# Laying out the scores and messages of an edge pass with the window's slots innermost

## The chip, the cores and the metric

The program runs on one core of one Trainium2 chip. The metric is device time in microseconds (us); the median of three runs of the kernel before is 3240.64 us (3236.63 to 3243.51). Engines are named as the profile names them: PE (TensorE matmul), PEld (its weight load), DVE (VectorE), ACT (ScalarE), POOL (GpSimd), SP (SyncE, which only issues transfers here).

## The reference

The model has two layers on x[128 graphs, 128 nodes, 128 features]: an attention layer over each graph, a mixture of 8 experts, a second attention layer, and a second mixture of 4 experts whose gates come from a graph attention over 524288 edges. Only that last gate is touched here:

```python
h = (x_flat @ W_gat).reshape(M, HEADS, NUM_EXPERTS)          # 4 heads x 4 experts
src = concatenate([edge_index[0], loops]); dst = concatenate([edge_index[1], loops])
a_src = (h * att_src).sum(-1); a_dst = (h * att_dst).sum(-1)
e = leaky_relu(a_src[src] + a_dst[dst], negative_slope=0.2)
e_max = segment_max(e, dst); ee = exp(e - e_max[dst])
denom = segment_sum(ee, dst); alpha = ee / (denom[dst] + 1e-16)
agg = segment_sum(h[src] * alpha[:, :, None], dst).reshape(M, 16) + b_gat
scores = layernorm(agg).reshape(M, HEADS, NUM_EXPERTS).mean(1)
# top 2 of 4 experts, softmax of their scores, weighted sum of gelu(x@W1+b1)@W2+b2
```

## The kernel before

Until about 1780 us of the span the kernel does both attention layers, the first mixture of experts and, between them on VectorE, a sort of all edges by destination. The rest is one function, `edges_and_experts1`, and all that changes lies in it.

After the sort, an edge's row has 20 floats: the 16 values h of its source (`GAT`) and the 4 scores a_src (`ROW` = 20 with them). A node's row `node[:, n, ROW:TAB]` has the 4 scores a_dst. Two pipelines run side by side.

*Gathers on POOL.* Edges are taken in parts of 2048, 16 per lane. `gather(u)` (L1508) issues 16 indirect transfers per part, each fetching one edge row for each of the 128 lanes into `edge_rows`; SP writes a finished part to the DRAM table `edge_table` in sorted order. POOL's loop does two parts (32 gathers), and then `windows` (L1514): two more indirect transfers that fetch for each lane a *window*, 40 consecutive sorted edge rows (`WINDOW` = 40), for each of two node pairs, into `win[P, 2, 40*20]`. POOL issues in order. The two window transfers wait for `picked` and `win_free`, which VectorE gives during the turn before.

*Turns on VectorE.* One `turn` handles a unit of 4 rows per lane (`UNIT` = 4: two pairs with two mates each, `PAIRS` = `MATES` = 2). It waits for its window, then: L1381 adds the two score terms into `sc`; L1383 to L1390 apply the leaky relu and put -1e30 on slots outside a row's edges (`hide`); L1393 takes the maximum over the 40 slots; L1400 subtracts it; ScalarE takes exp (L1594, waits for `scored`, gives `exped`); L1407 multiplies h by the weights into `msg`; L1411 and L1416 sum weights and messages over the slots; L1417 to L1458 make the gates from small tiles; L1470 adds up the four experts' outputs, which TensorE and ScalarE have made in the meantime (L1636, L1590, L1640, L1643). There are 32 turns. The first 31 each wait for windows that POOL fetches between gathers; the gathers have ended when the 31st runs, and its window transfers are followed by those of the last, 32nd turn, which POOL issues once `win_free` is given after L1416 has been issued.

In `sc` the order before is row, slot, head, and in `msg` row, slot, column, so the sums and maxima over slots read every 4th or every 16th float. The order of instructions on each engine is as written; no scheduler moves them. `step` adds to a semaphore, `settle` waits until all steps so far are done, `then` is both.

Of the kernel before, what the change touches and what calls it, by code (L numbers as in the profile page):

```python
# [6 lines left out]
ALU = mybir.AluOpType  # L7
# [5 lines left out]
AX_X = mybir.AxisListType.X  # L13

P = 128
# [27 lines left out]
HEADS = 4  # L43
TOP_EXPERTS = 4
GAT = HEADS * TOP_EXPERTS
ROW = GAT + HEADS
TAB = ROW + HEADS
WINDOW = 40
# [4 lines left out]
UNIT = 4  # L53
UNITS = GRAPHS // UNIT
MATES = 2
PAIRS = UNIT // MATES
# [9 lines left out]
BIG = 1e30  # L66
# [1085 lines left out]
def edges_and_experts1(nc, sem, a, x, rstd, shift, node, found, counted, source_ids, row_id, table_dram, edges_dram, out, ident, ones):  # L1152
# [5 lines left out]
    E = TOP_EXPERTS  # L1158
    SPAN = UNIT * NODES
    ROOT_GUESS = float(0x5F3759DF)  # L1160
    with ExitStack() as ctx:
        def sb(name, shape, dt=F32):
            return ctx.enter_context(nc.sbuf_tensor(name, shape, dt))
# [16 lines left out]
        win, win_ids = sb("win", [P, PAIRS, WINDOW * ROW]), sb("win_ids", [P, PAIRS], U32)  # L1180
# [4 lines left out]
        sc, hide = sb("win_score", [P, UNIT, WINDOW, HEADS]), sb("win_hide", [P, UNIT, WINDOW])  # L1185
        newtop, fade = sb("win_top", [P, UNIT, HEADS]), sb("win_fade", [P, UNIT, HEADS])
        msg, got, sums, adv = sb("win_msg", [P, UNIT, WINDOW, GAT]), sb("win_got", [P, UNIT, GAT]), sb("win_sums", [P, UNIT, HEADS]), sb("win_adv", [P, PAIRS])
# [50 lines left out]
        def _(dve):  # L1238
# [106 lines left out]
            FULL, HALF_FULL = [P, UNIT, WINDOW, HEADS], [P, PAIRS, WINDOW, HEADS]  # L1345
            w = win[:, :, :].rearrange("p t (k c) -> p t k c", c=ROW)
            w_flat = win[:, :, :].rearrange("p t (k c) -> p (t k) c", c=ROW)
            flat = sc[:, :, :, :].rearrange("p t k h -> p (t k h)")
            by_head = sc[:, :, :, :].rearrange("p t k h -> p t h k")
# [11 lines left out]
            def turn(came, unit, theirs, after):  # L1361
                mine, pair, after = bass.ds(unit * UNIT, UNIT), bass.ds(unit * PAIRS, PAIRS), bass.ds(after * PAIRS, PAIRS)
                mates = [bass.ds(unit * UNIT + m * PAIRS, PAIRS) for m in range(MATES)]
# [3 lines left out]
                def step(ins):  # L1367
                    ins.then_inc(step_s, 1)
                    done[0] += 1
# [4 lines left out]
                def then(ins):  # L1374
                    step(ins)
                    settle()
# [3 lines left out]
                for m in range(MATES):  # L1380
                    step(dve.tensor_tensor(sc[:, m * PAIRS:(m + 1) * PAIRS, :, :], w[:, :, :, GAT:ROW],  # L1381
                                           node[:, mates[m], ROW:TAB].unsqueeze(2).to_broadcast(HALF_FULL), ALU.add))
# [7 lines left out]
                step(dve.scalar_tensor_tensor(sc[:, :, :, :], hide[:, :, :].unsqueeze(3).to_broadcast(FULL), -BIG, sc[:, :, :, :], ALU.mult, ALU.add))  # L1390
                step(dve.tensor_scalar(adv[:, :], left[:, last_mates], 0.0, float(WINDOW), ALU.is_gt, ALU.mult))
                settle()
                step(dve.tensor_reduce(newtop[:, :, :], by_head, AX_X, ALU.max))  # L1393
# [6 lines left out]
                step(dve.tensor_tensor(sc[:, :, :, :], sc[:, :, :, :], newtop[:, :, :].unsqueeze(2).to_broadcast(FULL), ALU.subtract))  # L1400
# [4 lines left out]
                for m in range(MATES):  # L1405
                    of_mate = slice(m * PAIRS, (m + 1) * PAIRS)
                    step(dve.tensor_tensor(msg[:, of_mate, :, :].rearrange("p t k (h e) -> p (t k) h e", h=HEADS),  # L1407
                                           w_flat[:, :, 0:GAT].rearrange("p k (h e) -> p k h e", h=HEADS),
                                           sc[:, of_mate, :, :].rearrange("p t k h -> p (t k) h").unsqueeze(3).to_broadcast([P, PAIRS * WINDOW, HEADS, E]),
                                           ALU.mult))  # L1410
                step(dve.tensor_reduce(sums[:, :, :], by_head, AX_X, ALU.add))  # L1411
# [4 lines left out]
                step(dve.tensor_reduce(got[:, :, :], msg[:, :, :, :].rearrange("p t k c -> p t c k"), AX_X, ALU.add))  # L1416
# [407 lines left out]
```

## Time and profile before

| | us |
|---|---|
| median of 3 runs | 3240.64 |
| profiled execution, its own time | 3238.14 |
| its span, first to last instruction | 3236.1 |
| DVE busy | 2264.2 |
| PE busy | 1841.2 |
| POOL busy | 1806.9 |
| ACT busy | 1207.0 |
| 32 turns begin at 1875.26 and end with the span | 1360.8 |

The profile is of one execution. Its page lists the busy time of each engine, then groups of instructions; the trace behind it can be asked for groups by line and form, for waits (who was idle, and what ended it), for single lines, and for a timeline of one engine, where the start and the length of each instruction stand. Adjacent instructions of one line are merged there (x2), and a number in brackets is the idle time ahead.

### The profile page before, as it was taken

What the parts mean: (1) busy time and instruction counts of PE and PEld (TensorE: products, weight loads), DVE (VectorE), ACT (ScalarE), POOL (GpSimd) and SP (SyncE); (2) the same over time, 40 slices, a digit from 0 to 9 for tenths busy, and PEclk for the clock granted to TensorE, in tenths of its full rate; (3) what the DMA queues carried; (4) which work ended last, traced back from release to release, by engine and by line L of the source; (5) the groups of instructions that cost most, each with busy time, mean ns of one, the idle gap of its engine ahead of it and who ended that gap; (6) DMA issues with size and microseconds to landing.
All of it is one profiled execution on the core that took longest, in us unless ns stands there. A gap on an engine that the chain in (4) does not pass through costs nothing. (4 is left out here: it accounts for less than half of the span.)

```text
span 3236.1 us, 31753 instructions
## 1 busy us (share of the span) xinstructions
PE 1841.2 (57%) x9062; PEld 1287.2 (40%) x9117; DVE 2264.2 (70%) x4413; ACT 1207.0 (37%) x2449; POOL 1806.9 (56%) x1723
## 2 busy tenths in 40 slices
PE   0687764207777776366895325555555555545455
PEld 0466664205555444256785113322232333222233
DVE  7698978698888789977772355565666555656666
ACT  2576775414443433144783112222222222222222
POOL 4200024863544434254676777777777777777771
PEclk9998885559998988677895667777777777777777
DMA  6992000100111110121111111222112212221221
GB/s 236 291 393 106 4 19 24 39 27 23 39 46 32 45 39 14 49 67 49 48 36 35 34 40 41 43 43 41 32 41 43 43 41 43 43 41 30 43 43 34
DMA packets 169701, 192.40 MB, mean 59 GB/s; under 512 B 59193, under 2 KB 126048, under 8 KB 168960
## 3 DMA queue, kind: packets, MB, share of 16 engines
q1 hardware_dynamic: 107184, 118.69, 11.1%
q0 software_dynamic: 57088, 62.48, 9.5%
q10 hardware_dynamic: 5328, 9.97, 0.8%
q8 instruction: 52, 0.85, 0.1%
q14 instruction: 49, 0.40, 0.0%
HBM read 91.70 MB, written 105.25 MB: 61 GB/s over the span
## 5 line engine op out<-in xcount | busy, mean ns | idle before, releaser
L1508 POOL DMA_INDIRECT edge_rows<-node_table,edge_ids x1024 | 992.5, 969 | 313.5 <-issue 288.0
L1135 POOL DMA_INDIRECT token_results<-arena,token_of x160 | 247.9, 1550 | 362.6 <-ACT arena L1065 273.1
L579 DVE TENSOR_TENSOR sort_ping<-sort_pong 128x2048 f32<-128x2048 f32 (+1 forms) x238 | 407.1, 1751 | 48.1 <-ACT sort_pong L1003 43.4
L579 DVE TENSOR_TENSOR sort_pong<-sort_ping 128x2048 f32<-128x2048 f32 (+1 forms) x238 | 407.0, 1751 | 39.9 <-ACT sort_ping L1003 35.4
L1128 POOL DMA_INDIRECT slots<-arena,send x128 | 179.2, 1400 | 420.7 <-ACT arena L1022 385.3
L1630 PE MATMUL x_b_featT<-ident,x_feat 128*128 128x128 f32 x128 | 34.8, 428 | 630.3 <-PEq L1233 630.3
L1148 POOL DMA_INDIRECT adjacent<-keys,row_ids x256 | 249.2, 974 | 179.5 <-issue 78.9
L1381 DVE TENSOR_TENSOR win_score<-win,masked 128x320 f32<-128x320 f32 x64 | 28.6, 489 | 452.7 <-DMA win<-edge_table,win_ids 451.5
L1636 PE MATMUL x_b_hid<-x_featT,x_w 128*128 128x512 f32 x512 | 310.1, 759 | 28.3 <-PEq L1233 28.3
L1643 PEld LDWEIGHTS x_b_res<-x_w,x_hid 128*128 128x128 f32 x2048 | 243.5, 195 | 97.2 <-issue 97.2
L1630 PEld LDWEIGHTS x_b_featT<-ident,x_feat 128*128 128x128 f32 x128 | 22.9, 217 | 635.7 <-issue 635.7
L1643 PE MATMUL x_b_res<-x_w,x_hid 128*128 128x128 f32 x2048 | 268.3, 285 | 0.0
L89 ACT ACTIVATE arena<-x,shift,rstd 128x128 f32<-128x128 f32 x512 | 210.0, 485 | 109.8 <-DMA slots<-arena,send 86.2
L1590 ACT ACTIVATE x_hid<-x_b_hid,x_b 128x512 f32<-128x512 f32 x256 | 175.9, 687 | 120.5 <-PE x_b_hid L1636 120.5
L1636 PEld LDWEIGHTS x_b_hid<-x_featT,x_w 128*128 128x128 f32 x512 | 107.1, 238 | 217.6 <-ACT x_hid L1590 126.3
L1597 ACT ACTIVATE w_taken<-w_taken 128x16 f32<-128x16 f32 x32 | 6.9, 216 | 494.7 <-ACTq L1233 494.7
L1594 ACT ACT_TABLE_LOAD x32 | 41.1, 1283 | 352.8 <-ACTq L1233 352.8
L1640 PE MATMUL x_b_res<-x_b,ones 1*128 1x512 f32 x256 | 143.2, 639 | 27.8 <-PEq L1233 27.8
L958 PEld LDWEIGHTS banks<-arena 128*128 128x128 f32 x1280 | 145.9, 192 | 30.3 <-issue 30.3
L958 PE MATMUL banks<-arena 128*128 128x128 f32 x1280 | 153.5, 278 | 0.0
L949 PE MATMUL banks<-arena 128*128 128x512 f32 x320 | 149.3, 611 | 1.8 <-issue 1.8
L248 PE MATMUL banks<-ones,arena 128*128 128x1 f32 x512 | 84.5, 234 | 113.3 <-DVE x L276 61.2
(341 smaller groups left out, 4206.1 us busy)
## 6 DMA issues: line engine op xcount, KB each, us to landing
edge_table<-zeros SPq DMA_DIRECT2D x8, 5120.0 KB, 35.5
edge_rows<-node_table,edge_ids POOLq DMA_INDIRECT x1024
arena<-slots SPq DMA_DIRECT2D x40, 260.0 KB, 2.7
slots<-zeros SPq DMA_DIRECT2D x2, 5120.0 KB, 23.6
edge_table<-edge_rows SPq DMA_DIRECT2D x64, 160.0 KB, 1.8
out_dram<-x_y ACTq DMA_DIRECT2D x33, 256.0 KB
adjacent<-in_adj_dram SPq DMA_DIRECT2D x32, 256.0 KB, 2.7
arena<-token_results SPq DMA_DIRECT2D x32, 256.0 KB, 2.8
```

The costliest lines, as they stand in the source:

```text
L89: last = act.activation(out[:, u, :], x[:, bass.ds(b, 1), :].rearrange("p o f -> p (o f)"), ACT.Identity, bias=shift[:, bass.ds(b, 1)], sc ...
L579: step(dve.tensor_tensor(vb[:, :, t, :], va[:, :, 0, :], va[:, :, 1, :], op))
L949: pe.matmul(b_hid[:, at % 3, :], w1[:, e % 2, c * P:(c + 1) * P], rowsT[:, m % 2, :], start=True, stop=True).then_inc(hid_mm, 1)
L958: last = pe.matmul(b_res[:, n % 2, r, :], hid[:, n % 2, c, r * P:(r + 1) * P], w2[:, e % 2, c, :], start=False, stop=(r == PER - 1 and c = ...
L1128: pool.indirect_dma_start(slots_dram, bass.IndirectOffsetOnAxis(send[:, q:q + 1], 0), sent_feat[:, n % 2, v, :], None, bounds_check=EXPERT ...
L1135: pool.indirect_dma_start(rows_dram, bass.IndirectOffsetOnAxis(token_of[:, n % 4, r:r + 1], 0), res[:, n % 2, r, :], None, bounds_check=TO ...
L1148: pool.indirect_dma_start(fetched[:, n % 2, c, :], None, keys_dram, bass.IndirectOffsetOnAxis(row_ids[:, q:q + 1], 0)).then_inc(fetched_s[ ...
L1508: pool.indirect_dma_start(rows[:, u, c, :], None, table_dram, bass.IndirectOffsetOnAxis(ids[:, u, c:c + 1], 0)).then_inc(rows_in[u], 16)
L1590: act.activation(hid[:, c, :], b_hid[:, c % 2, :], ACT.Gelu, bias=b1[:, c:c + 1]).then_inc(hid_s, 1)
L1636: pe.matmul(b_hid[:, c % 2, :], w1[:, c // HC1, c % HC1 * P:(c % HC1 + 1) * P], featT[:, :], start=True, stop=True).then_inc(hid_mm, 1)
L1640: pe.matmul(b_res[:, e, :, :], ones[0:1, :], b2[0:1, e, :].unsqueeze(1).to_broadcast([1, UNIT, FEAT]), start=True, stop=False)
L1643: last = pe.matmul(b_res[:, e, v, :], hid[:, e * HC1 + c, v * P:(v + 1) * P], w2[:, e * HC1 + c, :], start=False, stop=(v == UNIT - 1 and ...
```

## The change

`sc` is laid out as row, head, slot and `msg` as row, column, slot. What reads or writes them follows:

```diff
-        sc = sb("win_score", [P, UNIT, WINDOW, HEADS])
+        sc = sb("win_score", [P, UNIT, HEADS, WINDOW])
-        msg = sb("win_msg", [P, UNIT, WINDOW, GAT])
+        msg = sb("win_msg", [P, UNIT, GAT, WINDOW])
...
                 for m in range(MATES):
-                    step(dve.tensor_tensor(sc[:, m * PAIRS:(m + 1) * PAIRS, :, :], w[:, :, :, GAT:ROW],
-                                           node[:, mates[m], ROW:TAB].unsqueeze(2).to_broadcast(HALF_FULL), ALU.add))
+                    step(dve.tensor_tensor(sc[:, m * PAIRS:(m + 1) * PAIRS, :, :], w[:, :, :, GAT:ROW].rearrange("p t k h -> p t h k"),
+                                           node[:, mates[m], ROW:TAB].unsqueeze(3).to_broadcast(HALF_FULL), ALU.add))
...
-                step(dve.scalar_tensor_tensor(sc[:, :, :, :], hide[:, :, :].unsqueeze(3).to_broadcast(FULL), -BIG, sc[:, :, :, :], ALU.mult, ALU.add))
+                then(dve.tensor_scalar(hide[:, :, :], hide[:, :, :], -BIG, None, ALU.mult))
+                step(dve.tensor_tensor(sc[:, :, :, :], sc[:, :, :, :], hide[:, :, :].unsqueeze(2).to_broadcast(FULL), ALU.add))
...
-                step(dve.tensor_reduce(newtop[:, :, :], by_head, AX_X, ALU.max))
+                step(dve.tensor_reduce(newtop[:, :, :], sc[:, :, :, :], AX_X, ALU.max))
...
-                for m in range(MATES):
-                    of_mate = slice(m * PAIRS, (m + 1) * PAIRS)
-                    step(dve.tensor_tensor(msg[:, of_mate, :, :].rearrange("p t k (h e) -> p (t k) h e", h=HEADS),
-                                           w_flat[:, :, 0:GAT].rearrange("p k (h e) -> p k h e", h=HEADS),
-                                           sc[:, of_mate, :, :].rearrange("p t k h -> p (t k) h").unsqueeze(3).to_broadcast([P, PAIRS * WINDOW, HEADS, E]),
-                                           ALU.mult))
-                step(dve.tensor_reduce(sums[:, :, :], by_head, AX_X, ALU.add))
+                for v in range(UNIT):
+                    step(dve.tensor_tensor(msg[:, v, :, :].rearrange("p (h e) k -> p h e k", h=HEADS),
+                                           w[:, v % PAIRS, :, 0:GAT].rearrange("p k (h e) -> p h e k", h=HEADS),
+                                           sc[:, v, :, :].unsqueeze(2).to_broadcast([P, HEADS, E, WINDOW]), ALU.mult))
+                step(dve.tensor_reduce(sums[:, :, :], sc[:, :, :, :], AX_X, ALU.add))
...
-                step(dve.tensor_reduce(got[:, :, :], msg[:, :, :, :].rearrange("p t k c -> p t c k"), AX_X, ALU.add))
+                step(dve.tensor_reduce(got[:, :, :], msg[:, :, :, :], AX_X, ALU.add))
```

The window `win` itself keeps its layout, since transfers fill it row by row: it is now read with the slot innermost, every 20th float. In the changed kernel's line numbers L1381 becomes L1379, L1390 becomes L1388 and L1389, L1393 becomes L1392, L1400 becomes L1399, L1407 becomes L1405, L1411 becomes L1408 and L1416 becomes L1413.

On VectorE, at the scores of a turn, the order before is:

```order
L1381 TENSOR_TENSOR win_score<-win,masked 128x320
L1383 ISA
L1383 TENSOR_TENSOR win_hide<-window_order,left 128x160
L1386 SCALAR_TENSOR_TENSOR win_score<-win_score 128x640
L1387 SCALAR_TENSOR_TENSOR win_hide<-win_hide 128x80
L1388 TENSOR_SCALAR left<-left 128x4
L1390 SCALAR_TENSOR_TENSOR win_score<-win_hide,win_score 128x640
```

and now (`masked` is the memory in which `node` lies):

```order
L1379 TENSOR_TENSOR win_score<-win,masked 128x320
L1381 ISA
L1381 TENSOR_TENSOR win_hide<-window_order,left 128x160
L1384 SCALAR_TENSOR_TENSOR win_score<-win_score 128x640
L1385 SCALAR_TENSOR_TENSOR win_hide<-win_hide 128x80
L1386 TENSOR_SCALAR left<-left 128x4
L1388 TENSOR_SCALAR win_hide<-win_hide 128x160
L1389 TENSOR_TENSOR win_score<-win_score,win_hide 128x640
```

One instruction has been split in two, with a wait between; the rest stands where it stood. On VectorE, at the messages, before:

```order
L1402 TENSOR_SCALAR top<-win_top 128x16
L1407 TENSOR_TENSOR win_msg<-win,win_score 128x1280 x2
L1411 TENSOR_REDUCE win_sums<-win_score 128x16
L1412 REGISTER_ALU
L1412 TENSOR_TENSOR total<-total,win_fade 128x16
L1414 ISA
L1414 TENSOR_TENSOR acc<-acc,win_fade 128x64
L1416 TENSOR_REDUCE win_got<-win_msg 128x64
```

and now:

```order
L1401 TENSOR_SCALAR top<-win_top 128x16
L1405 TENSOR_TENSOR win_msg<-win,win_score 128x640 x4
L1408 TENSOR_REDUCE win_sums<-win_score 128x16
L1409 REGISTER_ALU
L1409 TENSOR_TENSOR total<-total,win_fade 128x16
L1411 ISA
L1411 TENSOR_TENSOR acc<-acc,win_fade 128x64
L1413 TENSOR_REDUCE win_got<-win_msg 128x64
```

Two products of 1280 have become four of 640. No other engine's order has changed.

## Rows read from the trace of the kernel before

**Rows 1.** The page: busy time of each engine over the span.

```profile
PE 1841.2 (57%) x9062; PEld 1287.2 (40%) x9117; DVE 2264.2 (70%) x4413; ACT 1207.0 (37%) x2449; POOL 1806.9 (56%) x1723
```

**Rows 2.** Waits from 1780 us on: total us, times, longest us.

```profile
DVE win_score L1381 <- DMA win<-edge_table,win_ids: 451.5, 31, 62.1
...
POOL edge_rows L1508 <- issue: 288.0, 945, 0.3
```

**Rows 3.** A stretch, line L1508 alone: from:to, length, POOL busy us (instructions).

```profile
1875.00:3163.60 1288.60, 924.42 (x958) 0.75 0.20 40
```

**Rows 4.** Line L1508: shortest, median, longest of its gathers in ns.

```profile
L1508 POOL DMA_INDIRECT edge_rows<-node_table,edge_ids x1024: 940/944/2745, 1784.3 to 3162.6; - x171
```

**Rows 5.** Timeline, VectorE, one turn: start us, length us, instruction.

```profile
2220.34 0.89 DVE L1381 TENSOR_TENSOR win_score<-win,masked 128x320 f32<-128x320 f32 x2 [12.06 <-DMA win<-edge_table,win_ids]
...
2221.50 0.82 DVE L1386 SCALAR_TENSOR_TENSOR win_score<-win_score 128x640 f32<-128x640 f32 x1
...
2228.76 2.89 DVE L1407 TENSOR_TENSOR win_msg<-win,win_score 128x1280 f32<-128x1280 f32 x2 [2.40 <-DVEq L1233]
2231.57 1.28 DVE L1411 TENSOR_REDUCE win_sums<-win_score 128x16 f32<-128x640 f32 x1
...
2233.15 4.42 DVE L1416 TENSOR_REDUCE win_got<-win_msg 128x64 f32<-128x2560 f32 x1
```

**Rows 6.** Timeline, GpSimd, the same turn.

```profile
2220.61 1.04 POOL L1508 DMA_INDIRECT edge_rows<-node_table,edge_ids  x1 [0.30 <-issue]
2221.95 1.19 POOL L1508 DMA_INDIRECT edge_rows<-node_table,edge_ids  x1 [0.30 <-issue]
...
2225.94 1.03 POOL L1508 DMA_INDIRECT edge_rows<-node_table,edge_ids  x1 [0.30 <-issue]
...
2228.52 0.94 POOL L1508 DMA_INDIRECT edge_rows<-node_table,edge_ids  x1 [0.30 <-issue]
2229.77 1.30 POOL L1508 DMA_INDIRECT edge_rows<-node_table,edge_ids  x1 [0.30 <-issue]
2231.38 1.09 POOL L1508 DMA_INDIRECT edge_rows<-node_table,edge_ids  x1 [0.30 <-issue]
...
2234.02 0.94 POOL L1508 DMA_INDIRECT edge_rows<-node_table,edge_ids  x1 [0.30 <-issue]
```

**Rows 7.** Timeline, VectorE, before the turns begin.

```profile
1806.26 2.29 DVE L1338 TENSOR_TENSOR acc<-masked,self_w 128x2048 f32<-128x2048 f32 x1
```

**Rows 8.** Timeline, GpSimd, the same moment.

```profile
1806.62 2.75 POOL L1508 DMA_INDIRECT edge_rows<-node_table,edge_ids  x1 [0.30 <-issue]
```

**Rows 9.** Groups by line and form, VectorE: busy us, mean ns, idle before.

```profile
L1416 DVE TENSOR_REDUCE win_got<-win_msg 128x64 f32<-128x2560 f32 x32 | 141.5, 4422 | 1.1
...
L1407 DVE TENSOR_TENSOR win_msg<-win,win_score 128x1280 f32<-128x1280 f32 x64 | 92.7, 1490 | 77.9 <-DVEq L1233 77.9
...
L1393 DVE TENSOR_REDUCE win_top<-win_score 128x16 f32<-128x640 f32 x32 | 41.5, 1296 | 1.1
L1411 DVE TENSOR_REDUCE win_sums<-win_score 128x16 f32<-128x640 f32 x32 | 40.5, 1266 | 0.0
...
L1381 DVE TENSOR_TENSOR win_score<-win,masked 128x320 f32<-128x320 f32 x64 | 28.6, 489 | 452.7 <-DMA win<-edge_table,win_ids 451.5 <-DVEq L1233 1.2
...
L1400 DVE TENSOR_TENSOR win_score<-win_score,win_top 128x640 f32<-128x640 f32 x32 | 26.2, 818 | 0.0
...
L805 DVE TENSOR_REDUCE counts<-adjacent 128x8 f32<-128x512 f32 x32 | 22.0, 686 | 1.1
...
L629 DVE TENSOR_SCALAR sort_ping<-sort_pong,sort_sense 128x2048 f32<-128x2048 f32 x8 | 10.3, 1286 | 0.3
...
L703 DVE TENSOR_TENSOR counts<-banks,found 128x256 f32<-128x256 f32 x4 | 2.5, 612 | 0.1
```

**Rows 10.** Timeline, VectorE, the last turn.

```profile
3207.59 0.17 DVE L1402 TENSOR_SCALAR top<-win_top 128x16 f32 x1
```

**Rows 11.** Timeline, ScalarE, the last turn.

```profile
3209.15 1.28 ACT L1594 ACT_TABLE_LOAD   x1 [0.30 <-ACTq L1233]
```

More of the change, by code:

```diff
@@ L1184, in edges_and_experts1 @@
         order_i, order = sb("window_order_i", [P, WINDOW], I32), sb("window_order", [P, WINDOW])
-        sc, hide = sb("win_score", [P, UNIT, WINDOW, HEADS]), sb("win_hide", [P, UNIT, WINDOW])
+        sc, hide = sb("win_score", [P, UNIT, HEADS, WINDOW]), sb("win_hide", [P, UNIT, WINDOW])
         newtop, fade = sb("win_top", [P, UNIT, HEADS]), sb("win_fade", [P, UNIT, HEADS])
-        msg, got, sums, adv = sb("win_msg", [P, UNIT, WINDOW, GAT]), sb("win_got", [P, UNIT, GAT]), sb("win_sums", [P, UNIT, HEADS]), sb("win_adv", [P, PAIRS])
+        msg, got, sums, adv = sb("win_msg", [P, UNIT, GAT, WINDOW]), sb("win_got", [P, UNIT, GAT]), sb("win_sums", [P, UNIT, HEADS]), sb("win_adv", [P, PAIRS])
         gat_b, gamma, beta = sb("gat_b", [P, GAT]), sb("gat_gamma", [P, GAT]), sb("gat_beta", [P, GAT])
@@ L1343, in _ @@
             dve.wait_ge(weights_in, 64)
-            FULL, HALF_FULL = [P, UNIT, WINDOW, HEADS], [P, PAIRS, WINDOW, HEADS]
+            FULL, HALF_FULL = [P, UNIT, HEADS, WINDOW], [P, PAIRS, HEADS, WINDOW]
             w = win[:, :, :].rearrange("p t (k c) -> p t k c", c=ROW)
-            w_flat = win[:, :, :].rearrange("p t (k c) -> p (t k) c", c=ROW)
-            flat = sc[:, :, :, :].rearrange("p t k h -> p (t k h)")
-            by_head = sc[:, :, :, :].rearrange("p t k h -> p t h k")
+            flat = sc[:, :, :, :].rearrange("p t h k -> p (t h k)")
             A, B = agg[:, :, :], square[:, :, :]
@@ L1399, in turn @@
                 step(dve.tensor_tensor(fade[:, :, :], top[:, mine, :], newtop[:, :, :], ALU.subtract))
-                step(dve.tensor_tensor(sc[:, :, :, :], sc[:, :, :, :], newtop[:, :, :].unsqueeze(2).to_broadcast(FULL), ALU.subtract))
+                step(dve.tensor_tensor(sc[:, :, :, :], sc[:, :, :, :], newtop[:, :, :].unsqueeze(3).to_broadcast(FULL), ALU.subtract))
                 settle()
```

## The prediction, on record before the changed kernel ran

> **What bounds the kernel now.** I read the page's busy times first, then the waits of the last stage, then the timelines of VectorE and GpSimd side by side. By busy time VectorE looks like the bound (2264.2 of 3236.1 us [rows 1]), and the change edits only VectorE. But the edit sits in the turns, and there VectorE is the one that waits: 31 of 32 turns begin with idle time that a window transfer ends, 451.5 us in all, 62.1 of it ahead of the first turn [rows 2], so (451.5 - 62.1) / 30 = 13.0 us a turn. In the turn shown it was 12.06 [rows 5]. GpSimd does not pause: of its gaps between gathers, 945 come to 288.0 us, 0.30 each, and the longest is 0.3 [rows 2]. A turn therefore lasts as long as GpSimd takes for 32 gathers and 2 window transfers, 34 x (0.944 + 0.304) = 42.4 us, and whatever prolongs a gather goes straight into the kernel's time, while up to 12 us on VectorE go nowhere.
>
> What prolongs gathers is the finding on which all else rests. Their shortest and median are 940 and 944 ns, the longest 2745 [rows 4]. From 1875 to 3163.6 us, 958 gathers took 924.42 us [rows 3]; at 0.944 each they would take 904.4, so 20.0 us, or 0.67 us in each of 30 turns, is excess. Side by side the timelines say where it falls. A gather that began 0.45 us into L1386 took 1.19 us, one that began 1.01 us into the first L1407 took 1.30, and the next, in the second L1407, 1.09 [rows 5, 6]. L1338 is the clearest: it began at 1806.26 and lasted 2.29; the gather that began at 1806.62 took 2.75, 1.81 more than the median [rows 7, 8]. In all these cases the gather went on 0.12 us before the VectorE instruction's recorded end (1808.55 against 1806.62 + 1.81 = 1808.43; 2230.24 against 2229.77 + 0.36 = 2230.13). These instructions read two tensors from SBUF. The sum L1416 reads one, and the gather that began 0.87 us into it took 0.94 [rows 5, 6]: it holds nothing. So the price of a two-tensor instruction is how long it holds the gather that starts under it, and a reduction has no price outside the last turns.
>
> The Trainium skill (SBUF — State Buffer, section SBUF: two separate sides) says that VectorE and GpSimd share a port pair as an exclusive lock for a whole instruction, which a VectorE instruction takes in a two-port mode or with two SBUF inputs. The trace agrees for two inputs, by the 2.75 us above.
>
> **VectorE, part by part.** Lengths come from groups [rows 9]. Contiguous reads: 512 elements 686 ns, 640 elements 818, so 1.04 ns an element plus about 153. Strided ones cost more: L1416 (every 16th float) (4422 - 153) / 2560 = 1.67 ns; L1411 and L1393 (every 4th) 1.74 and 1.79; L703, a product with both inputs strided, (612 - 153) / 256 = 1.79. L1407 and L1381 read runs of four floats and pay 1.04.
>
> - Reductions become contiguous: L1392 and L1408 820 ns each in place of 1296 and 1266, -0.48 and -0.45 us; L1413 153 + 2667 = 2820 ns in place of 4422, -1.60.
> - The window is now what is read with a stride, every 20th float. No row shows a product with one input like this. Bounds: 1.04 ns (as L1407 now) and, above the strided rows, 2.1. I take 1.73, the mean of 1.67, 1.74 and 1.79. L1379: 153 + 554 = 707 ns in place of 489, two of them, +0.44.
> - L1405: 153 + 1107 = 1260 ns. Before, the pair took 2.81 us from its start to that of L1411 [rows 5], 1.405 each, 0.085 less than its recorded 1.490; now each steps by 1.175, and four take 4.70. +1.89.
> - L1388, a product of 160 with a constant, and its wait: L629 shows 0.55 ns an element for that form, at most 160 x 1.04 + 153 = 320 ns; I take +0.27 (0.2 to 0.35).
>
> Sum per turn: -0.48 - 0.45 - 1.60 + 0.44 + 1.89 + 0.27 = +0.07 us. With 1.04 ns for the window it is -2.0 us; with 2.1 it is +1.3. What the sums gain the products lose.
>
> The page on the microarchitecture (Vector Engine (DVE) Microarchitecture Reference, section Measured stream behaviour on trn2) of the Trainium skill states that a port keeps its full rate only on runs of two or more adjacent words; its table has 1.73 ns for one source that hops at every element and 2.50 for two sources stepping 24 words. This speaks against the change, and by 1.73 the sum is the one above. By 2.50 a turn would be 2.6 us longer on VectorE.
>
> In turns 1 to 30 this sum is hidden by the 12 us of idle time. The last two turns have no gathers after them: turn 31 begins on its window and turn 32 follows at once, so their VectorE time is the kernel's end. Turn 31 gives +0.07. In turn 32 the score part (+0.44 + 0.27 - 0.48 = +0.23) falls into a wait: L1402 ended at 3207.76 and ScalarE began only at 3209.15 [rows 10, 11], kept by its own gelus. What remains there is +1.89 - 0.45 - 1.60 = -0.16. The tail is -0.1 us, nothing.
>
> **The holds.** This is where the time moves. Before, the L1407 pair costs 0.36 + 0.15 = 0.51 us in the turn shown [rows 6], and the score instructions 0.10 + 0.25 + 0.09. Now walk a gather through four products that step by 1.175 and release a held gather at 1.260 - 0.12 = 1.14 after their start. Today a gather starts at 2228.52, 0.24 us before L1407, and goes free; the next starts 1.01 in. The products will start 0.23 later, so that gather is 0.78 into the first one and is held 0.36; averaged over all phases a first hold is 1.14² / 2 / 1.248 = 0.52. I take 0.4. Once released, the next gather starts 0.944 + 0.304 = 1.248 later, 2.39 after the product's start, and the third product starts at 2.35: it arrives 0.04 after that start and is held 1.10. If it slips in just ahead, the one after it starts at 3.64 against the fourth product's 3.525 and is held 1.03. Either way a second hold of 1.05. So 1.45 in place of 0.51: +0.94. The two L1379 hold for 0.59 in place of 0.37 of their length; mean hold of both, 2 x L² / 2 / 1.248, goes from 0.11 to 0.28, of which I take +0.1 since a gather held there shifts the later ones. Together +1.05 us a turn, 30 turns: **+31.5 us**.
>
> 3238.14 + 31.5 - 0.1 = 3269.5 us on the profiled execution's own time. The median of the runs is 2.5 above that execution, so 3272 us.
>
> **Rivals.**
> 1. *The steps mesh.* With r ns an element a held gather is followed by one that starts 640r + 0.033 + 1.248 us after the product's start, and the third product starts at 1280r + 0.136. From r = 1.79 on the gather is ahead of it, and then of the fourth as well, so only the first hold is left: at 1.85 ns some 0.6 to 0.7 in place of 0.51, with the scores +0.2 a turn, +6: 3247. For: 1.79 is in two rows. Against: the long sums are at 1.67 and 1.74. 18%.
> 2. *The strided product costs nothing* (other side: not slower). L1407's four-float runs at 1.04 ns show that a product need not pay for every jump. Then products step by 0.74, hold for 0.70 and the total of holds stays near 0.67 a turn, while the tail gives 2 x -2.0 = -4: 3236. It decides below about 1.15 ns. Against it stands L703, a product at 1.79. 9%.
> 3. *Dear strides or bad phases.* At 2.1 ns and more the products hold 1.38 us each, twice or three times, and even at 1.67 a long first hold can be followed by a second and a long one at the scores: +1.9 a turn, 57 us, and a tail of 3: 3300. This is also the time that the skill's 2.50 ns would give, though no row here reaches it. 10%.
> 4. *Gathers are not held by this form*, or the excess has a cause that I misread: 3241. 5%.
>
> **How the numbers follow.** The forecast has 58%, its own range 3256 to 3290 (0.6 to 1.7 us a turn). A measurement of this kernel tells a change of about 0.2%, 6.5 us, from none. Slower by more: 58 + 10 + half of rival 1, 77%. Within: half of rival 1, most of 2, and 4, 18%. Faster: 5%. The range for 8 in 10 goes from rival 1's lower half to rival 3: 3241 to 3303.
>
> **What the changed profile would show.** L1405 near 1.26 us, L1379 near 0.71, L1413 near 2.82, L1392 and L1408 near 0.82; VectorE still idle 11 to 13 us ahead of a turn; gathers with a mean near 1.00 us in place of 0.969, some of 1.9 to 2.0 us under L1405; starts of turns some 44 us apart. It would be wrong if L1405 took 0.82 us (rival 2), or if turns were no further apart though L1405 takes 1.26 (rivals 1 and 4).

## The result, and the profile after

The changed kernel takes 3249.39 us (median of 14 runs), the kernel before 3240.67 us (14 runs): ratio 1.0025, 95% interval 1.0017 to 1.0034. It got slower by 8.7 us. One of the changed kernel's 14 runs took 3627.44 us in a slower state and the ratio leaves it out; without it the median is 3248.96, 0.4 us less, which changes nothing below. I had forecast slower, but by 31.5 us.

The changed kernel's groups on VectorE (busy us, mean ns), which answer to [rows 9]:

```profile
L1405 DVE TENSOR_TENSOR win_msg<-win,win_score 128x640 f32<-128x640 f32 x128 | 174.9, 1428 | 77.5 <-DVEq L1233 77.5
...
L1413 DVE TENSOR_REDUCE win_got<-win_msg 128x64 f32<-128x2560 f32 x32 | 90.2, 2820 | 1.1
...
L1379 DVE TENSOR_TENSOR win_score<-win,masked 128x320 f32<-128x320 f32 x64 | 47.9, 790 | 440.5 <-DMA win<-edge_table,win_ids 439.3 <-DVEq L1233 1.2
...
L1389 DVE TENSOR_TENSOR win_score<-win_score,win_hide 128x640 f32<-128x640 f32 x32 | 26.4, 826 | 1.1
...
L1392 DVE TENSOR_REDUCE win_top<-win_score 128x16 f32<-128x640 f32 x32 | 26.2, 820 | 1.1
...
L1408 DVE TENSOR_REDUCE win_sums<-win_score 128x16 f32<-128x640 f32 x32 | 25.9, 808 | 0.0
...
L1388 DVE TENSOR_SCALAR win_hide<-win_hide 128x160 f32<-128x160 f32 x32 | 7.8, 243 | 1.1
```

The reductions came out as forecast: 2820 and 820 ns, and 808 for the weights. The mask's product took 243 ns. The two instructions that read the window did not: 640 elements at step 20 took 1428 ns, (1428 - 153) / 640 = 1.99 ns an element in place of the 1.73 I took, and L1379 took 790 ns in place of 707, again 1.99.

VectorE still waits ahead of each turn (this row answers to [rows 2]), (439.3 - 61.9) / 30 = 12.6 us:

```profile
DVE win_score L1379 <- DMA win<-edge_table,win_ids: 439.3, 31, 61.9
```

The gathers' busy time in 958 gathers of the turns, which answers to [rows 3]:

```profile
1879.00:3178.20 1299.20, 934.14 (x958) 0.74 0.20 40
```

934.14 against 924.42 us: 29.8 us of excess over 0.944 each in place of 20.0, or 0.99 a turn in place of 0.67. That is +9.7 us.

The two profiled spans differ by 15.2 us, 3251.3 against 3236.1. 4.1 of that lies ahead of the first turn, in code that is the same (it begins at 1879.37 in place of 1875.26), 10.1 in the time from the start of one turn to that of the next (43.50 in place of 43.17 us, 30 times), and 1.0 in the last two turns (66.8 us from the start of the 31st in place of 65.8). The medians' 8.7 us is the second and third of these within the scatter of the runs.

One turn of the changed kernel, on VectorE:

```profile
2487.69 1.50 DVE L1379 TENSOR_TENSOR win_score<-win,masked 128x320 f32<-128x320 f32 x2 [12.27 <-DMA win<-edge_table,win_ids]
...
2489.45 0.83 DVE L1384 SCALAR_TENSOR_TENSOR win_score<-win_score 128x640 f32<-128x640 f32 x1
...
2496.55 5.46 DVE L1405 TENSOR_TENSOR win_msg<-win,win_score 128x640 f32<-128x640 f32 x4 [2.39 <-DVEq L1233]
```

and on GpSimd:

```profile
2488.58 1.36 POOL L1505 DMA_INDIRECT edge_rows<-node_table,edge_ids  x1 [0.30 <-issue]
2490.25 1.00 POOL L1505 DMA_INDIRECT edge_rows<-node_table,edge_ids  x1 [0.30 <-issue]
...
2496.55 0.94 POOL L1505 DMA_INDIRECT edge_rows<-node_table,edge_ids  x1 [0.30 <-issue]
2497.80 0.94 POOL L1505 DMA_INDIRECT edge_rows<-node_table,edge_ids  x1 [0.30 <-issue]
2499.04 1.04 POOL L1505 DMA_INDIRECT edge_rows<-node_table,edge_ids  x1 [0.30 <-issue]
2500.39 1.04 POOL L1505 DMA_INDIRECT edge_rows<-node_table,edge_ids  x1 [0.30 <-issue]
2501.73 1.04 POOL L1505 DMA_INDIRECT edge_rows<-node_table,edge_ids  x1 [0.30 <-issue]
```

The four products step by (5.46 - 1.43) / 3 = 1.34 us. A gather started with the first one and was free; the next started 1.25 in, as the product was ending, and was free too. The third met the second product 1.15 in and was held 0.10, and then the fourth and fifth were held 0.10 as well. That is one pattern, not three accidents: a gather's cycle is 1.248 us and a product's 1.345, so a held gather is followed by one that starts at the same point of the next product, and each is held for the difference, 0.10. No gather here meets a product at its beginning, where a hold costs over 1 us. Added up over 30 turns from such timelines, gathers under the products have 0.28 us of excess a turn, where the pair before had 0.44. The scores cost more, 0.72 us a turn (gathers that start in a turn's first 6 us) in place of 0.21: by the instruction that holds them, L1384 went from 0.06 to 0.38 and the pair of L1379 from 0.07 to 0.25. In the turn shown it is 0.42 + 0.06; two turns earlier, GpSimd and then VectorE:

```profile
2399.93 1.20 POOL L1505 DMA_INDIRECT edge_rows<-node_table,edge_ids  x1 [0.30 <-issue]
2401.44 1.54 POOL L1505 DMA_INDIRECT edge_rows<-node_table,edge_ids  x1 [0.30 <-issue]
```

```profile
2399.58 1.49 DVE L1379 TENSOR_TENSOR win_score<-win,masked 128x320 f32<-128x320 f32 x2 [11.56 <-DMA win<-edge_table,win_ids]
...
2401.34 0.82 DVE L1384 SCALAR_TENSOR_TENSOR win_score<-win_score 128x640 f32<-128x640 f32 x1
```

One gather was held 0.26 by the pair of L1379, and so the next started 0.10 into the long L1384 and was held 0.60.

### The profile page after: what moved, and what is told of

Same layout as the page of the kernel before. It is cut to its first block and busy times, and to the rows that moved or that the text cites. A ratio compares the mean times of both kernels' runs of the same rounds, so it can differ in the third digit from the quotient of the medians.

```text
span 3251.3 us, 31904 instructions
## 1 busy us (share of the span) xinstructions
PE 1852.0 (57%) x9117; PEld 1292.7 (40%) x9117; DVE 2287.2 (70%) x4509; ACT 1207.3 (37%) x2449; POOL 1816.3 (56%) x1723
## 5 line engine op out<-in xcount | busy, mean ns | idle before, releaser
L1379 DVE TENSOR_TENSOR win_score<-win,masked 128x320 f32<-128x320 f32 x64 | 47.9, 790 | 440.5 <-DMA win<-edge_table,win_ids 439.3
L1633 PE MATMUL x_b_hid<-x_featT,x_w 128*128 128x512 f32 x512 | 310.9, 761 | 28.3 <-PEq L1233 28.3
L1405 DVE TENSOR_TENSOR win_msg<-win,win_score 128x640 f32<-128x640 f32 x128 | 174.9, 1428 | 77.5 <-DVEq L1233 77.5
```

Of the source, the lines that this page charges most:

```text
L1405: step(dve.tensor_tensor(msg[:, v, :, :].rearrange("p (h e) k -> p h e k", h=HEADS), w[:, v % PAIRS, :, 0:GAT].rearrange("p k (h e) -> p h ...
L1633: pe.matmul(b_hid[:, c % 2, :], w1[:, c // HC1, c % HC1 * P:(c % HC1 + 1) * P], featT[:, :], start=True, stop=True).then_inc(hid_mm, 1)
```

## Experiments

Two theories were on record for all of them. *Excess* is what the gathers take beyond 0.944 us each. P, for phase: what a two-tensor instruction costs is how far into it the next gather starts, so the step of these instructions against 1.248 us decides. B, for busy share: the excess is about a tenth of the time that VectorE spends in such instructions. Before and after fit both.

Two batches ran where the kernel before took 3240.58 and 3241.93 us, as in the result. Three batches ran on chips where it took 3724.0 to 3757.4 us; I call them the long batches, and they come last.

**Products at step 16 (msg_step16_b).** The products read the window at step 16 in place of 20, so they multiply other values and give other messages, in the same shapes.

```diff
-  w[:, v % PAIRS, :, 0:GAT].rearrange("p k (h e) -> p h e k", h=HEADS)
+  win[:, v % PAIRS, 0:WINDOW * 16].rearrange("p (k c) -> p k c", c=16)[:, :, 0:GAT].rearrange("p k (h e) -> p h e k", h=HEADS)
```

> msg_step16 again, because in its first run GpSimd stood still between its loops for transfers that landed late (361 us in all, also in every other kernel of that batch), which covers differences of some tens of us. Theory P (phase): excess of the gathers about 2.5 us a turn against 0.96 of the changed kernel, about 45 us slower than it, 1.7% over before. Theory B (busy share): excess 0.88, no slower than the changed kernel.

Measured: 3302.63 us against 3240.58 for before, ratio 1.0194 (1.0175 to 1.0213), that is 62 us slower than before and about 53 slower than the changed kernel, where P had 45. The products' group, and one turn on VectorE:

```profile
L1405 DVE TENSOR_TENSOR win_msg<-win,win_score 128x640 f32<-128x640 f32 x128 | 148.5, 1223 | 77.5 <-DVEq L1233 77.5
```

```profile
2511.89 1.49 DVE L1379 TENSOR_TENSOR win_score<-win,masked 128x320 f32<-128x320 f32 x2 [15.31 <-DMA win<-edge_table,win_ids]
...
2520.72 4.64 DVE L1405 TENSOR_TENSOR win_msg<-win,win_score 128x640 f32<-128x640 f32 x4 [2.40 <-DVEq L1233]
```

On GpSimd in that turn:

```profile
2520.71 0.94 POOL L1505 DMA_INDIRECT edge_rows<-node_table,edge_ids  x1 [0.30 <-issue]
2521.96 1.90 POOL L1505 DMA_INDIRECT edge_rows<-node_table,edge_ids  x1 [0.30 <-issue]
2524.17 1.97 POOL L1505 DMA_INDIRECT edge_rows<-node_table,edge_ids  x1 [0.30 <-issue]
2526.44 0.94 POOL L1505 DMA_INDIRECT edge_rows<-node_table,edge_ids  x1 [0.31 <-issue]
```

A product is 0.2 us shorter than in the changed kernel, (1223 - 153) / 640 = 1.67 ns an element, and the kernel is 53 us slower. The products step by 1.14 us. The gather of 2521.96 met the second product 0.10 in and was held 0.96 us. The next one, 2524.17, met the fourth (2520.72 + 3 x 1.14 = 2524.14) 0.03 in and was held 1.03. This is the second hold that the prediction had: its walk, with 1.73 ns, put it 0.04 into a later product. The first hold is another matter: the prediction took 0.4 for it, and here it is 0.96. Over 30 turns the gathers under the products have 1.98 us of excess a turn and those under the scores 0.88. VectorE meanwhile waited more, since it had less to do in a longer turn:

```profile
DVE win_score L1379 <- DMA win<-edge_table,win_ids: 518.7, 31, 62.1
```

Theory B said no slower than the changed kernel, and is out.

**The same work, shifted (sums_first_b).** The sum of the weights goes ahead of the products.

```diff
+  step(dve.tensor_reduce(sums[:, :, :], sc[:, :, :, :], AX_X, ALU.add))
   for v in range(UNIT):
       step(dve.tensor_tensor(msg[:, v, :, :], ...
-  step(dve.tensor_reduce(sums[:, :, :], sc[:, :, :, :], AX_X, ALU.add))
```

> sums_first again. P: the holds under the products grow from 0.3 to about 1.0 us a turn, excess 1.3 to 1.75 in all, 10 to 24 us slower than the changed kernel (ratio to before 1.006 to 1.010). B: same as the changed kernel (1.0025).

Measured: 3273.32 us, ratio 1.0107 (1.009 to 1.0124), 24 us slower than the changed kernel, the upper end of P's 10 to 24; B had no change. VectorE and GpSimd:

```profile
2500.57 5.45 DVE L1406 TENSOR_TENSOR win_msg<-win,win_score 128x640 f32<-128x640 f32 x4
```

```profile
2501.09 1.67 POOL L1505 DMA_INDIRECT edge_rows<-node_table,edge_ids  x1 [0.30 <-issue]
2503.06 1.04 POOL L1505 DMA_INDIRECT edge_rows<-node_table,edge_ids  x1 [0.30 <-issue]
```

A gather met the first product 0.52 in and was held 0.73. From there the pattern of 0.10 goes on. The four products do the same work, start 0.74 us later, behind an instruction that holds nothing, and cost 24 us more.

**Long instruction, no stride (before_merged_c).** The kernel before, its two products in one.

```diff
-  for m in range(MATES): step(dve.tensor_tensor(msg[:, of_mate, :, :]..., w_flat..., sc[:, of_mate, :, :]..., ALU.mult))
+  step(dve.tensor_tensor(msg[:, :, :, :].rearrange("p (m t) k (h e) -> p m (t k) h e", m=MATES, h=HEADS),
+       w_flat[...].unsqueeze(1).to_broadcast([P, MATES, PAIRS * WINDOW, HEADS, E]),
+       sc[:, :, :, :].rearrange("p (m t) k h -> p m (t k) h", m=MATES).unsqueeze(4).to_broadcast([...]), ALU.mult))
```

> before_merged a third time; in two batches GpSimd stood still for late transfers. P: one product of 2.83 us holds a gather for 1.6 to 1.7 us a turn, excess about 2.0 in place of 0.64, about 40 us slower than before, ratio 1.012. B: no change, ratio 1.000.

Measured: 3277.4 us against 3241.93, ratio 1.0112 (1.0095 to 1.0129), 35 us slower for one instruction fewer. P had 40, B none.

```profile
2504.00 2.85 DVE L1405 TENSOR_TENSOR win_msg<-win,win_score 128x2560 f32<-128x2560 f32 x1 [2.39 <-DVEq L1233]
```

```profile
2505.25 2.43 POOL L1506 DMA_INDIRECT edge_rows<-node_table,edge_ids  x1 [0.30 <-issue]
```

The gather that started 1.25 us in took 2.43 us, 1.49 too long. So a hold needs no stride. It needs a long instruction and a gather that starts well ahead of its end.

**Weights in PSUM (before_psum_b).** In the kernel before, ScalarE writes exp of the scores into two PSUM banks, and the products and sums read them there.

```diff
-  act.activation(sc[:, :, :, :], sc[:, :, :, :], ACT.Exp).then_inc(exped, 1)
+  for m in range(MATES):
+      act.activation(weights_of(m), sc[:, m * PAIRS:(m + 1) * PAIRS, :, :], ACT.Exp).then_inc(exped, 1)   # b_next, b_featT
```

> before_psum again for the same reason. P: excess 0.2 to 0.4 us a turn in place of 0.64, 8 to 13 us faster than before (ratio 0.996 to 0.9975). B: 0.36, 8 us faster. The holds under the products are gone in either (they were gone in the first run); the time is what is asked.

Measured: 3226.02 us, ratio 0.9962 (0.9948 to 0.9977), 15 us faster than before; P's 8 to 13 and B's 8 both lie in the interval, so the time does not tell the two apart. On VectorE the products are as long as ever, and on GpSimd:

```profile
2479.57 1.49 DVE L1411 TENSOR_TENSOR win_msg<-win,b_next 128x1280 f32<-128x1280 f32 x1 [2.49 <-DVEq L1233]
2480.98 1.48 DVE L1411 TENSOR_TENSOR win_msg<-win,x_b_featT 128x1280 f32<-128x1280 f32 x1
```

```profile
2479.25 0.94 POOL L1513 DMA_INDIRECT edge_rows<-node_table,edge_ids  x1 [0.30 <-issue]
2480.50 0.94 POOL L1513 DMA_INDIRECT edge_rows<-node_table,edge_ids  x1 [0.30 <-issue]
2481.74 0.95 POOL L1513 DMA_INDIRECT edge_rows<-node_table,edge_ids  x1 [0.30 <-issue]
```

The gathers that started 0.93 us into the first product and 0.76 into the second took 0.94 and 0.95 us. With one operand in PSUM nothing is held. This ties the holds to two SBUF inputs. The section of the Trainium skill that the prediction named (SBUF — State Buffer, SBUF: two separate sides) says that a VectorE instruction with at most one SBUF input, outside the two-port modes, does not contend with GpSimd, and the trace agrees by these two rows. It also reports a probe in which a tensor_tensor did not stall a DMA; here one does, by the 2.43 us above, and the measurement decides.

**The same in the changed kernel (after_psum_b).** The same edit, applied to L1405 and L1408.

> after_psum again. P: only the holds under the scores are left, excess about 0.64 us a turn, 10 us faster than the changed kernel, level with before (ratio 0.998 to 1.001). B: excess 0.41, ratio 0.998.

Measured: 3241.13 us, ratio 1.0006 (0.9996 to 1.0015): level with before, 8 us faster than the changed kernel. P's 0.998 to 1.001 holds; B's 0.998 lies outside the interval. What is left are the holds under the scores. With the holds gone from the products of both kernels, the old layout (0.9962) beats the new one (1.0006) by 15 us. The profiled executions show about half of it: 0.42 us of excess a turn against 0.60 (L1381 is shorter than L1379) is 5.5 us, and the last two turns take 65.3 us against 66.9. The rest I cannot place; this kernel's profiled execution, 3230.86 us, was the fastest of its ten.

**More operands in PSUM (before_psum_more_c).** Also the node scores, the mask and the new maxima are kept in `b_next`.

```diff
+  then(dve.tensor_copy(near[:, :, :], node[:, mine, ROW:TAB]))                    # near, hide_p, newtop: b_next
   came()
-  ... node[:, mates[m], ROW:TAB].unsqueeze(2)...
+  ... near[:, m * PAIRS:(m + 1) * PAIRS, :].unsqueeze(2)...
+  step(dve.tensor_copy(hide_p[:, 0:PAIRS, :], hide[:, 0:PAIRS, :]))
```

> before_psum_more a third time, for the same reason. P and B: excess 0.1 to 0.2 us a turn, about 3219, ratio 0.993 to 0.995, where transfers are on time; if they are late, 2% slower than before, as twice so far.

Measured: 3223.55 us against 3241.93, ratio 0.9943 (0.9927 to 0.996), the fastest here. P and B both had 0.993 to 0.995. The two intervals overlap, so the time alone does not show a gain over before_psum_b; the gathers' excess does, 0.14 us a turn in place of 0.42.

**All of them together.** The gathers' group in each profile, in the order changed kernel, msg_step16_b, sums_first_b, before_merged_c, before_psum_b, after_psum_b, before_psum_more_c (busy us, mean ns of 1024):

```profile
L1505 POOL DMA_INDIRECT edge_rows<-node_table,edge_ids x1024 | 1002.3, 979 | 313.0 <-issue 291.1 <-POOLq L1233 21.9
```

```profile
L1505 POOL DMA_INDIRECT edge_rows<-node_table,edge_ids x1024 | 1057.4, 1033 | 312.9 <-issue 289.5 <-POOLq L1233 22.5 <-DMA edge_table<-edge_rows 0.9
```

```profile
L1505 POOL DMA_INDIRECT edge_rows<-node_table,edge_ids x1024 | 1020.8, 997 | 312.7 <-issue 292.2 <-POOLq L1233 20.5
```

```profile
L1506 POOL DMA_INDIRECT edge_rows<-node_table,edge_ids x1024 | 1028.5, 1004 | 312.8 <-issue 290.1 <-POOLq L1233 22.6
```

```profile
L1513 POOL DMA_INDIRECT edge_rows<-node_table,edge_ids x1024 | 984.4, 961 | 313.1 <-issue 288.9 <-POOLq L1233 24.2
```

```profile
L1510 POOL DMA_INDIRECT edge_rows<-node_table,edge_ids x1024 | 989.1, 966 | 312.8 <-issue 291.9 <-POOLq L1233 20.8
```

```profile
L1518 POOL DMA_INDIRECT edge_rows<-node_table,edge_ids x1024 | 975.7, 953 | 313.8 <-issue 289.9 <-POOLq L1236 23.9
```

Before had 992.5 us by its page. Against the medians' differences to before on the same chip:

| kernel | gathers' busy us against 992.5 | time against before, us |
|---|---|---|
| changed kernel | +9.8 | +8.7 |
| msg_step16_b | +64.9 | +62.0 |
| sums_first_b | +28.3 | +32.7 |
| before_merged_c | +36.0 | +35.5 |
| before_psum_b | -8.1 | -14.6 |
| after_psum_b | -3.4 | +0.6 |
| before_psum_more_c | -16.8 | -18.4 |

The gathers' busy time accounts for all seven within 7 us. Single runs of the kernel before scatter by 10 (3233.85 to 3244.09), and the last two turns and the code ahead of the turns are not in it.

**The long batches.** The first runs of the first four kernels, and two batches with the others, fell on chips where the kernel before took 3724.0 to 3757.4 us. The texts on record speak of transfers that land late there. The traces show something else, as told below.

> The changed kernel with one edit: L1405 reads the window with every 16th float in place of every 20th, so it multiplies other values of the window than the right ones (same shapes, same count). Theory P (phase): a gather that starts under a two-tensor product is held until that product ends, and the next one starts 1.248 us later, so what counts is the product's step against 1.248 us. If a step of 16 costs 1.67 ns an element as L1416 of before did, the products step by 1.14 us in place of 1.345, a second hold of about 1.0 us comes back each turn, the excess of gathers over 0.944 us goes from 0.96 to about 2.5 us a turn, and the kernel gets about 45 us slower than the changed one (about 3295), though VectorE has 0.8 us less to do a turn. Theory B (busy share): the excess is a tenth of the time that VectorE spends in two-tensor instructions (0.64 us at 6.6 us before, 0.96 at 9.5 after); with 0.8 us less it is 0.88 a turn and the kernel 2 to 4 us faster than the changed one (about 3246).

> The changed kernel with the reduction of the weights (L1408, 0.81 us) issued ahead of the four products in place of behind them. VectorE's work is the same. Theory P: the products start 0.74 us later in the gathers' cycle of 1.248 us, the first hold gets longer and each later product catches the next gather again; excess 1.75 us a turn in place of 0.96, about 24 us slower than the changed kernel (about 3273). Theory B: same busy time, same excess, 3249 within 2 us.

> The kernel before, but ScalarE writes exp of the scores into two PSUM banks that are idle then (two instructions of 320 in place of one of 640), and the products L1407 and the sums L1411 (two of 320) read them there. So the products read one tensor from SBUF and one from PSUM. Both theories: no hold under the products; the excess goes from 0.64 to about 0.2 us a turn (P) or 0.36 (B, with 2.8 us less of two-tensor time), 13 us faster than before (P, about 3227) or 8 us (B, about 3232). If holds have nothing to do with SBUF's ports, 3241 within 2.

> The changed kernel with exp of the scores in PSUM in the same way. The products L1405 hold nothing any more; what is left are the holds under the scores, above all under L1379. P: excess 0.64 us a turn, 10 us faster than the changed kernel (about 3239). B: two-tensor time falls by 5.4 us of 9.5, excess 0.41, 16 us faster (about 3233).

Measured (before 3724.03): ratios 1.0132 (1.0095 to 1.0169), 1.0269, 1.023 and 1.0275, in this order. All four times are off, P's and B's alike.

> before_psum, and more operands in PSUM: the 16 node scores of a unit (copied there ahead of the wait for the window), the mask of slots and the new maxima. The score sum, the masking and the subtraction of the maxima then read one tensor from SBUF each; the leaky relu and the comparison that makes the mask still read two. P: excess 0.1 to 0.2 us a turn in place of 0.37 to 0.5, 5 to 9 us faster than before_psum, about 3219 (ratio to before 0.993 to 0.995). The added copies of 0.2 us on VectorE count twice at the end only. B: two-tensor time falls from 3.8 to 1.4 us, 7 us faster as well.

> The kernel before, with the two products L1407 of 1280 elements merged into one of 2560 (rows of both mates, the window read twice by a step of 0 over mates), contiguous rates as before. P: one instruction of 2.8 us holds any gather under it once, for 1.4 us on average and, by the phases seen (a gather starts 1.0 us in), for 1.7: excess about 2.0 us a turn in place of 0.64, about 40 us slower than before (ratio 1.012). B: two-tensor time the same but for 0.07 us: no change (ratio 1.000).

> The changed kernel, with L1379 iterating row, slot, head as before: it reads the window in runs of four floats and writes the scores with a step of 40 floats. It asks what a strided write costs: 320 elements in 0.49 us if nothing, about 0.79 if as much as the read at step 20. P: if it costs nothing the scores hold less (0.6 to about 0.2 us a turn) but the gathers then meet the products in another phase, and the excess stays at 0.9 to 1.1: no faster than the changed kernel (ratio to before 1.001 to 1.0035). B: two-tensor time falls by 0.6 us, 2 us faster than the changed kernel.

> The changed kernel with the products reading every 18th float of the window (other values than the right ones). It asks how the price of an element depends on the step: 1.67 ns at 16, 1.99 at 20. If it goes by size, about 1.83 ns here; if it goes by whether the step in floats is a multiple of 16 or of 8, 1.99. P: at 1.83 the products step by 1.24 us, as long as a gather's cycle, so nearly all holds under them go and the excess falls to about 0.8 us; at 1.99 it is as in the changed kernel, 0.96. B: 0.9.

Measured (before 3757.4): 1.0217, 1.0005 (0.9975 to 1.0034), 1.0004 (0.9989 to 1.0018), and 3815.93 us in a single run.

> before_psum_more again: in its first run GpSimd stood still for late transfers (over 500 us in all). P: excess 0.1 to 0.2 us a turn, 5 to 9 us faster than before_psum, about 3219, ratio to before 0.993 to 0.995. B: the same.

> before_merged again for the same reason. P: one long product of 2.83 us holds a gather for 1.6 to 1.7 us a turn, excess about 2.0, 40 us slower than before, ratio 1.012. B: no change, ratio 1.000.

> scores_in_runs again. In the first run L1379 took 0.711 us in place of 0.790 (a strided write costs 1.74 ns an element, against 1.99 for the read at step 20). P: the scores end 0.16 us earlier and hold a little less; by the phases the excess stays at 0.8 to 1.0 us, ratio to before 1.000 to 1.0025. B: 0.95, ratio 1.0023.

> msg_step18 again. In the first run a product of 640 took 1.316 us, 1.82 ns an element, so the products step by about 1.235 us, just short of a gather's cycle of 1.248. P: a gather held by one product starts 0.05 us or less into the one after the next, or just ahead of it: excess 0.8 to 1.1 us a turn, or, where it falls just inside, up to 2; ratio between 1.000 and 1.002 with the first, 1.009 with the second. B: 0.9, ratio 1.002. Beside step 16 (1.67 ns, ratio 1.019) and step 20 (1.99 ns, ratio 1.0025) it shows how sharply the holds depend on the product's length.

Measured (before 3754.35): 1.0215, 1.0052 (1.0028 to 1.0076), 1.0028 (1.0012 to 1.0045), 1.0168 (1.0132 to 1.0204).

The expected times of before_psum_more and msg_step18 did not come out. before_merged, 1.2% slower by P and level by B, was level once and 0.5% slower once. scores_in_runs came out at or near what both theories had.

GpSimd stands still for hundreds of us in each of these runs. In msg_step18_b the waits ahead of gathers, and one of VectorE's waits, are:

```profile
POOL edge_rows L1505 <- POOLq L1233: 463.8, 38, 24.9
```

```profile
DVE x_weighed L1467 <- DVEq L1233: 341.7, 26, 17.8
```

In the kernel before the first of these came to 25.5 us in 79 waits, the longest 1.7 us, and in the changed kernel VectorE never waited more than 0.2 us there. The wait on GpSimd stands ahead of a group of 16 gathers, which may start only when SP has written the part that last filled their buffer to `edge_table`. For every second part SP issues that write only once VectorE has seen its window (`win_seen`, given as a turn starts). One such moment, on VectorE, SP and GpSimd:

```profile
3347.38 1.12 DVE L1467 SCALAR_TENSOR_TENSOR x_weighed<-x_b_res,gates,x 128x128 f32<-128x128 f32 x4 [13.50 <-DVEq L1233]
...
3355.35 1.50 DVE L1379 TENSOR_TENSOR win_score<-win,masked 128x320 f32<-128x320 f32 x2 [3.23 <-issue]
3355.37 0.35 SPq L1550 DMA_DIRECT2D edge_table<-edge_rows  x1
...
3358.03 0.95 POOL L1505 DMA_INDIRECT edge_rows<-node_table,edge_ids  x1 [16.04 <-POOLq L1233]
```

The write goes out 0.02 us after the turn has started, and GpSimd goes on 2.7 us after that start. All 29 of its waits over 3 us in the turns of this run, 460 us in all, end 2.7 us after a turn's start; in the traces of seven other runs of these batches 174 of 177 such waits do (2.7 or 2.8 us). So the transfer was not late; the turn was. It was late because VectorE had been idle for 13.50 us ahead of L1467, and ScalarE (12.98 us) and TensorE (12.49 us) stood idle at the same time. There the turns wait within themselves and the gathers wait for the turns, so what a gather loses no longer sets the time. What stops the three engines no run here shows, nor why the ratios differ as they do: before_psum, before_psum_more, after_psum and sums_first are 2% to 3% slower than before, the others less. No trace of the kernel before on such a chip was taken.

These runs are good for two things all the same. The lengths of instructions can be read: a product at step 18, and L1379 when it reads in runs and writes at step 40.

```profile
L1405 DVE TENSOR_TENSOR win_msg<-win,win_score 128x640 f32<-128x640 f32 x128 | 160.6, 1316 | 78.5 <-issue 69.5 <-DVEq L1233 6.2 <-ACT win_fade L1592 2.8
```

```profile
L1379 DVE TENSOR_TENSOR win_score<-win,masked 128x320 f32<-128x320 f32 x64 | 40.5, 711 | 161.2 <-issue 98.0 <-DMA win<-edge_table,win_ids 61.9 <-DVEq L1233 1.2
```

(1316 - 153) / 640 = 1.82 ns and (711 - 153) / 320 = 1.74 ns. And gathers still meet products. In msg_step18_b:

```profile
3304.90 5.02 DVE L1405 TENSOR_TENSOR win_msg<-win,win_score 128x640 f32<-128x640 f32 x4 [2.39 <-issue]
```

```profile
3305.01 1.99 POOL L1505 DMA_INDIRECT edge_rows<-node_table,edge_ids  x1 [0.30 <-issue]
3307.30 0.94 POOL L1505 DMA_INDIRECT edge_rows<-node_table,edge_ids  x1 [0.30 <-issue]
```

The products step by 1.235 us. A gather 0.11 into the first was held 1.05; the next started 0.07 ahead of the third product and went free. Over 30 turns the products hold 1.00 us a turn, nearly all of it in one gather. So at 1.82 ns an element the second hold is gone, at 1.67 it is there. What either kernel would take on the other chips was not measured.

## Why the prediction was wrong

- *What bounds the turns*: right on the chips of the result. VectorE waited 12.6 us a turn, and seven kernels' times follow their gathers within 7 us. The rows also have 79 gaps between gathers that the text does not count, 25.5 us in all and at most 1.7; they are much the same in the changed kernel (21.9 us) and move nothing.
- *What holds a gather*: right. Two SBUF inputs, released a little ahead of the recorded end (0.13 us under the products of before, 0.19 under the new ones); PSUM operands took it away.
- *The reductions*: right to 2%.
- *The window's price*: the step that failed. "No row shows a product with one input like this ... I take 1.73, the mean of 1.67, 1.74 and 1.79." It is 1.99. The rows it was averaged from have other steps (4 and 16 floats in the reductions), and I treated the price as one number for any stride, while step 16 costs 1.67, 18 costs 1.82 and 20 costs 1.99. My bounds, 1.04 and 2.1, held it; my middle did not.
- *The walk through four products*: the second hold was right for its input, and the input was wrong. With 1.73 ns the walk has a second hold 0.04 us into a later product; msg_step16_b, at 1.67 ns, shows one of 1.03 us at 0.03, and msg_step18_b, at 1.82, shows none. With 1.99 the products step by 1.345 us, over a gather's 1.248, and the holds shrink to the difference. The term "1.45 in place of 0.51" measured 0.28 in place of 0.44 over the turns.
- *The first hold*: a second mistake, which the result hides. I took 0.4, near the mean over all phases. But the phase is set by what the gather met before, and comes out nearly the same each turn: in msg_step16_b a gather starts 0.10 us into a product in every one of the 30 turns and is held 0.96. That kernel, nearest to the rate I forecast with, lost 62 us and not 31.5: 1.98 us a turn under the products in place of 1.45, and 0.88 under the scores. It is what rival 3 said of long first holds (57 us). So with the rate right my size would probably still have been wrong.
- *Rival 1*, the steps that mesh, said +6 us in all and is what happened, but its sum is in part luck: it had the products go from 0.51 us a turn to 0.6 or 0.7, where they fell to 0.28, and left 0.1 or less for the scores, where 0.51 came on top.
- *The scores*: forecast +0.1 us a turn, measured +0.51. L1379 is longer than I took (0.790 us, not 0.707), and a gather held by it can be led into L1384, whose change I had put at nothing: of the +0.51, 0.32 lie under L1384. Over 30 turns the scores alone would be 15 us; the products gave 5 back, and 9.7 are left.
- *The tail*: forecast -0.1, measured +1.0. The rate again: per turn four products take 2.6 us more, two L1379 0.6 and the mask 0.27, against 2.5 saved. (Two small slips: with 1.04 ns the sum of a turn is -2.1 and not -2.0, and with 2.50 it is +2.5 and not 2.6. Nothing hangs on them.)
- The sum's sign was right, the size 3.6 times too large. The sign is partly luck too: the +1.05 us a turn was to come from the products, and they got cheaper; it came from the scores. The step that failed is one price, 1.73 ns in place of 1.99, on the wrong side of a threshold that lies between 1.67 and 1.82 by the runs. I had placed that threshold at 1.79 and given its other side 18%.

## What to carry to other kernels

Where GpSimd's descriptor work sets the pace, look at VectorE only for what stands in its way: two-tensor instructions with both inputs in SBUF, and of these the long ones and those whose step lies just under the gather's cycle. Put one operand in PSUM before changing layouts; it gave 15 to 18 us on the chips of the result, and cost 2% in the long batches, so measure on more than one chip. A layout that makes the reads of reductions contiguous moves the stride to whatever reads the shared source, so price that at its own step, and where the outcome has a threshold in it, weigh both sides of it over the whole of the bounds and do not go by the mean. And do not average a hold over all phases when both loops repeat: it falls at nearly the same phase each turn.

## What the runs showed of the hardware that I had not expected

- A strided read's price on VectorE depends on the step, and not in one direction: 1.74 to 1.79 ns an element at 4 floats (reductions), 1.67 at 16, 1.82 at 18, 1.99 at 20 (products), 1.04 in runs of four. A write at step 40 floats costs 1.74.
- In PSUM the stride of 4 costs nothing: the sums of before_psum_b read every 4th float there, and (484 - 153) / 320 = 1.03 ns an element where SBUF had 1.74.

```profile
L1416 DVE TENSOR_REDUCE win_sums<-b_next 128x8 f32<-128x320 f32 x32 | 15.5, 484 | 0.0
```

- A gather that starts with a two-tensor instruction, or just ahead of it, goes free (2496.55 above); one 0.03 us in was held 1.03 us. Over all gathers the edge lies about 0.02 us in.
- Shorter products made the changed kernel slower by 53 us, the same instructions in another order by 24; an instruction fewer made the kernel before slower by 35.
- The same kernel takes 3241 us on some chips and 3724 to 3757 on others. In the traces of the other kernels there, VectorE, ScalarE and TensorE stand idle together within a turn (12 to 14 us in the one shown), and GpSimd's waits end 2.7 us after the next turn starts. The cause is open.
